# A graph attention edge loop: two PSUM banks in turn for a step's z and its sums, leaky relu as a maximum, transposes in place of identity matmuls

## The reference, cut to what matters

```python
h = relu(layernorm(x))                     # 6250 x 256
xm = h @ W_n2m.T;  ea = edge_attr @ W_r2m.T
# one more loop per node, with the mean of its edges' ea as attribute
xl = xm @ Wl.T + bl;  xr = xm @ Wr.T + br  # 6250 x 128
e = ea_f @ We.T
u = leaky_relu(xl[src_f] + xr[dst_f] + e, 0.2)     # per edge, 8 heads x 16
logits = einsum('ehd,hd->eh', u, att)
alpha = softmax of logits over the edges of one target
out = segment_sum(xl[src_f] * alpha, dst_f) + bias
return x + out @ W_m2n.T
```

## Time and profile before

| | us |
|---|---|
| median of 3 runs | 2426.31 (2423.69 to 2429.64) |
| profiled execution, its own time | 2422.78 |
| its span, first to last instruction | 2421.0 |
| its mean granted TensorE clock | 0.974 of 2.4 GHz |

### The profile page before, as it was taken

How to read it: one execution, slowest core, us unless ns; L and a number is a source line. 1 busy time by engine, 2 the same in 40 slices (tenths; PEclk the granted TensorE clock), 3 DMA queues, 4 the chain that set the end, 5 groups by cost and what they waited for, 6 DMA issues and landing times. The chain is left out here.

```text
span 2421.0 us, 67070 instructions
## 1 busy us (share of the span) xinstructions
PE 2223.0 (92%) x14421; PEld 1609.4 (66%) x14422; DVE 1492.1 (62%) x4173; ACT 1339.9 (55%) x3905; POOL 1722.4 (71%) x1914
## 2 busy tenths in 40 slices
PE   3978999999999999999999999999899999999978
PEld 2745766667766776677666766776677667766656
DVE  4734666656665666566655665666566556666677
ACT  2714555556555655565555655665565556655553
POOL 3777777777777777777777777777777777777501
PEclk9969999999999999999999999999999999999989
DMA  6244444444444444444444544544455445444317
GB/s 200 82 113 112 115 118 111 111 111 121 112 111 112 120 112 110 114 120 113 109 115 114 116 109 115 118 114 108 115 117 114 107 115 118 115 109 112 72 41 134
DMA packets 323471, 272.65 MB, mean 113 GB/s; under 512 B 176135, under 2 KB 294568, under 8 KB 322786
## 3 DMA queue, kind: packets, MB, share of 16 engines
q1 hardware_dynamic: 256686, 144.01, 24.7%
q0 software_dynamic: 60704, 120.20, 21.5%
q10 hardware_dynamic: 5652, 3.68, 0.5%
HBM read 256.21 MB, written 19.40 MB: 114 GB/s over the span
## 5 line engine op out<-in xcount | busy, mean ns | idle before, releaser
L782 POOL DMA_INDIRECT xl_g<-xl_table,src_tab x1708 | 1638.0, 959 | 522.9 <-issue 518.0
L989 DVE SCALAR_TENSOR_TENSOR uT<-banks,relu 128x256 f32<-128x256 f32 x854 | 349.4, 422 | 529.8 <-issue 486.9
L852 PE MATMUL banks<-msg,onehot 128*128 128x177 f32 x3416 | 639.3, 330 | 6.2 <-DVE msg L979 2.3
L902 ACT ACTIVATE relu<-banks 128x256 f32<-128x256 f32 x854 | 319.0, 382 | 582.8 <-PE banks L807 548.5
L852 PEld LDWEIGHTS banks<-msg,onehot 128*128 128x128 f32 x3416 | 522.8, 192 | 172.6 <-issue 163.6
L807 PE MATMUL banks<-ident,xl_g 128*128 128x128 f32 x3416 | 507.1, 293 | 92.1 <-DMA xl_g<-xl_table,src_tab 89.9
L807 PEld LDWEIGHTS banks<-ident,xl_g 128*128 128x128 f32 x3416 | 424.2, 195 | 246.5 <-DMA xl_g<-xl_table,src_tab 168.0
L890 ACT ACTIVATE distance<-iota_n,minus_slot 128x128 f32<-128x128 f32 x1708 | 540.7, 389 | 0.4
L798 PE MATMUL banks<-onehotT,xr_parts 128*128 128x256 bf16 x2562 | 357.4, 276 | 34.9 <-issue 18.1
L895 ACT ACTIVATE onehot<-distance 128x512 f32<-128x512 f32 x427 | 268.9, 630 | 113.1 <-PE banks L852 93.8
L798 PEld LDWEIGHTS banks<-onehotT,xr_parts 128*128 x2562 | 246.0, 98 | 89.4 <-issue 45.3
(11 more groups left out here) (195 smaller groups left out, 1393.9 us busy)
## 6 DMA issues: line engine op xcount, KB each, us to landing
slot_bc<-slot_dram SPq DMA_DIRECT2D x427, 128.0 KB
xl_g<-xl_table,src_tab POOLq DMA_INDIRECT x1708
attrT<-in_attr_cols SPq DMA_DIRECT2D x854, 32.0 KB
rbf<-in_edge_attr SPq DMA_DIRECT2D x854, 32.0 KB
masks<-masks_dram SPq DMA_DIRECT2D x108, 96.5 KB
out<-in_x SPq DMA_DIRECT2D x16, 336.0 KB
out<-result POOLq DMA_DIRECT2D x6, 896.0 KB, 9.2
xl_table<-lr_sb SPq DMA_DIRECT2D x49, 64.0 KB, 1.5
```

What stands on the lines that cost most here:

```text
L782: pool.indirect_dma_start(out=xl_g[:, k % RING, t], out_offset=None, in_=xl_table, in_offset=bass.IndirectOffsetOnAxis(ap=src_tab[:, e:e + ...
L852: mm = nc.tensor.matmul(U_ps[h], onehot[:, j % 2, t], msg[:, j % 2, t], start=i == 0, stop=i == PT - 1)
L902: nc.scalar.activation(relu[:, h], z_ps[h], ACT.Relu, scale=1.0 - SLOPE).then_inc(relu_ready, 2 + h)
L989: nc.vector.scalar_tensor_tensor(out=uT[:, s % 2, h * PIECE:(h + 1) * PIECE], in0=z_ps[h], scalar=SLOPE, in1=relu[:, h], op0=ALU.mult, op1 ...
```

## The change

- z has one bank of 512 columns a step, two banks in turn. Its first matmul waits for z_copied of the step two back.
- The attributes of both pieces lie on the same 32 partitions, and one matmul of 512 columns takes them.
- The gathered rows are turned with is_transpose, still added into z. The finale's turns the same.
- ACT copies z to SBUF (z_copy, two in turn); DVE makes u = max(0.2 z, z) of it, both operands the copy, one operation of 512 columns.
- U of a step has one bank for both pieces, two in turn; the sums are added at SUM_LAG = LAG + 2 instead of LAG + 1, RESCALE moves from turn 9 to 10, and there is one more turn. TensorE waits for the sums of the step two back.
- The ring of slot_bc has 4 steps instead of 8. Semaphores that counted halves now count steps.

```diff
-SRING = 8
+SRING = 4
 LAG = BATCH + 9
+SUM_LAG = LAG + 2
...
-        attrT = sb("attrT", [SPLIT * D_RBF, TRING, PIECE])
-        relu = sb("relu", [P, SPLIT, PIECE])
+        attrT = sb("attrT", [D_RBF, TRING, GROUP])
+        z_copy = sb("z_copy", [P, 2, GROUP])
...
-        z_ps = [banks[:, h, 0:PIECE] for h in range(SPLIT)]
+        z_ps = [banks[:, par] for par in (0, 1)]
...
-        U_ps = banks[:, 2, P:P + AGG], banks[:, 5, 0:AGG]
+        U_ps = [banks[:, 2 + 3 * par, 0:SPLIT * AGG].rearrange("p (h c) -> p h c", h=SPLIT) for par in (0, 1)]
...
-        FORTH, BACK, ENDS, CHAIN, SPREAD, RAISE, TURN, SCALE, RESCALE = 1, 2, 3, 4, 5, 6, 7, 8, 9
+        FORTH, BACK, ENDS, CHAIN, SPREAD, RAISE, TURN, SCALE, RESCALE = 1, 2, 3, 4, 5, 6, 7, 8, 10
...
+                    z = z_ps[s % 2]
                     pe.wait_ge(ohT_ready, k + 1)
+                    if inside(k - 2, STEPS):
+                        pe.wait_ge(z_copied, k - 1)
                     for h in range(SPLIT):
-                        if inside(k - 1, STEPS):
-                            pe.wait_ge(u_ready, Z * (k - 1) + (2, Z)[h])
                         for part in range(PARTS):
-                            nc.tensor.matmul(z_ps[h], parts_of(xr_parts, w[h], part),
-                                             onehotT[:, n4, h * PIECE:(h + 1) * PIECE], start=part == 0, stop=False)
+                            nc.tensor.matmul(z[:, h * PIECE:(h + 1) * PIECE], parts_of(xr_parts, w[h], part),
+                                             onehotT[:, n4, h * PIECE:(h + 1) * PIECE],
+                                             start=h == 0 and part == 0, stop=False)
...
-                    for h in range(SPLIT):
-                        q = slice(h * D_RBF, (h + 1) * D_RBF)
-                        nc.tensor.matmul(z_ps[h], Wc[q], attrT[q, s % TRING], start=False, stop=False)
+                    nc.tensor.matmul(z, Wc[0:D_RBF], attrT[:, s % TRING], start=False, stop=False)
                     pe.wait_ge(gathers[s % RING], (r * (UNROLL // RING) + s // RING + 1) * GATHERED)
                     for h in range(SPLIT):
                         for i in range(PT):
-                            mm = nc.tensor.matmul(z_ps[h][:, i::PT], xl_g[:, s % RING, i * SPLIT + h], ident[:],
-                                                  start=False, stop=i == PT - 1)
-                        mm.then_inc(z_done, 2 + h)
+                            mm = nc.tensor.matmul(z[:, h * PIECE + i:(h + 1) * PIECE:PT], xl_g[:, s % RING, i * SPLIT + h],
+                                                  ident[:], start=False, stop=h == SPLIT - 1 and i == PT - 1,
+                                                  is_transpose=True)
+                    mm.then_inc(z_done, 1)
...
+                    if inside(k - LAG - 2, STEPS):
+                        pe.wait_ge(added, TICK * (k - LAG - 1))
                     for h in range(SPLIT):
-                        if inside(k - LAG - 1, STEPS):
-                            pe.wait_ge(added, TICK * (k - LAG - 1) + (1, TICK)[h])
...
-                    for h in range(SPLIT):
-                        act.wait_ge(z_done, Z * k + (2, Z)[h])
-                        if inside(k - 1, STEPS):
-                            act.wait_ge(u_ready, Z * (k - 1) + (2, Z)[h])
-                        nc.scalar.activation(relu[:, h], z_ps[h], ACT.Relu, scale=1.0 - SLOPE).then_inc(relu_ready, 2 + h)
+                    act.wait_ge(z_done, k + 1)
+                    if inside(k - 2, STEPS):
+                        act.wait_ge(u_ready, k - 1)
+                    nc.scalar.activation(z_copy[:, s % 2], z_ps[s % 2], ACT.Copy).then_inc(z_copied, 1)
...
-                a = k - LAG - 1
+                a = k - SUM_LAG
...
-                    dve.wait_ge(agg_done, TICK * a + 1)
+                    dve.wait_ge(agg_done, a + 1)
...
-                    for h in range(SPLIT):
-                        dve.wait_ge(relu_ready, Z * k + (2, Z)[h])
-                        if h == 0 and inside(k - 2, STEPS):
-                            dve.wait_ge(L_done, k - 1)
-                        nc.vector.scalar_tensor_tensor(out=uT[:, s % 2, h * PIECE:(h + 1) * PIECE], in0=z_ps[h],
-                                                       scalar=SLOPE, in1=relu[:, h], op0=ALU.mult, op1=ALU.add
-                                                       ).then_inc(u_ready, 2 + h)
+                    dve.wait_ge(z_copied, k + 1)
+                    if inside(k - 2, STEPS):
+                        dve.wait_ge(L_done, k - 1)
+                    z = z_copy[:, s % 2]
+                    nc.vector.scalar_tensor_tensor(out=uT[:, s % 2], in0=z, scalar=SLOPE, in1=z,
+                                                   op0=ALU.mult, op1=ALU.max).then_inc(u_ready, 1)
...
-                    nc.tensor.matmul(T_ps[:, i], old[:, b % 2, i], ident[:], start=True, stop=False)
-                    mm = nc.tensor.matmul(T_ps[:, i], own[:, b % 2, i], ident[:], start=False, stop=True)
+                    nc.tensor.matmul(T_ps[:, i], old[:, b % 2, i], ident[:], start=True, stop=False,
+                                      is_transpose=True)
+                    mm = nc.tensor.matmul(T_ps[:, i], own[:, b % 2, i], ident[:], start=False, stop=True,
+                                      is_transpose=True)
```

More of the change, by code:

```diff
@@ L705, in edge_loop @@
         FULL, GATHERED = SPLIT * 16, TILES * 16
-        (set_up, acc_zero, ohT_ready, node_saved, z_done, relu_ready, u_ready, L_done, dist_ready, oh_ready,
+        (set_up, acc_zero, ohT_ready, node_saved, z_done, z_copied, u_ready, L_done, dist_ready, oh_ready,
          attr_ready, msg_ready, agg_done, added, forth_done, run_done, ends_done, seq_ready, seq_half, seq_done,
@@ L709, in edge_loop @@
          last_ready, weight_ready, wT_done, spread_done, factor_ready, rescaled, x_set) = map(sem, (
-             "set_up", "acc_zero", "ohT_ready", "node_saved", "z_done", "relu_ready", "u_ready", "L_done",
+             "set_up", "acc_zero", "ohT_ready", "node_saved", "z_done", "z_copied", "u_ready", "L_done",
              "dist_ready", "oh_ready", "attr_ready", "msg_ready", "agg_done", "added", "forth_done", "run_done",
@@ L720, in edge_loop @@
         SET_UP, ACC_PARTS = 4, 7
-        TICK, Z = 3, 5
-        first, last_turn = -2, STEPS + LAG + 1
+        TICK = 3
+        first, last_turn = -2, STEPS + SUM_LAG
         looped = (4 * BATCH - 1, STEPS - 2)
-        FORTH, BACK, ENDS, CHAIN, SPREAD, RAISE, TURN, SCALE, RESCALE = 1, 2, 3, 4, 5, 6, 7, 8, 9
+        FORTH, BACK, ENDS, CHAIN, SPREAD, RAISE, TURN, SCALE, RESCALE = 1, 2, 3, 4, 5, 6, 7, 8, 10
         def batch_at(s, r, piece):
@@ L749, in _ @@
                     if inside(k - TRING, STEPS):
-                        sp.wait_ge(z_done, Z * (k - TRING + 1))
+                        sp.wait_ge(z_done, k - TRING + 1)
                         sp.sem_inc(z_seen, 1)
                     for h, e in enumerate(edges):
-                        sp.dma_start(attrT[h * D_RBF:(h + 1) * D_RBF, s % TRING], attr_cols[:, bass.DynSlice(e, PIECE)]
+                        sp.dma_start(attrT[:, s % TRING, h * PIECE:(h + 1) * PIECE], attr_cols[:, bass.DynSlice(e, PIECE)]
                                      ).then_inc(turned_in[s % TRING], 16)
@@ L846, in _ @@
                     pe.wait_ge(oh_ready, TICK * (k - LAG + 1))
+                    if inside(k - LAG - 2, STEPS):
+                        pe.wait_ge(added, TICK * (k - LAG - 1))
                     for h in range(SPLIT):
[L848 to L849 removed]
                         for i in range(PT):
                             t = i * SPLIT + h
[L852 removed]
+                            mm = nc.tensor.matmul(U_ps[j % 2][:, h], onehot[:, j % 2, t], msg[:, j % 2, t],
                                                   start=i == 0, stop=i == PT - 1)
[L854 removed]
+                    mm.then_inc(agg_done, 1)
                 b = batch_at(s, r, TURN)
@@ L893, in _ @@
                     if inside(k - LAG - 1, STEPS):
-                        act.wait_ge(agg_done, TICK * (k - LAG))
+                        act.wait_ge(agg_done, k - LAG)
                     nc.scalar.activation(onehot[:, m % 2], distance[:], ACT.Relu, scale=-1.0, bias=1.0
@@ L937, in _ @@
                         dve.wait_ge(acc_zero, ACC_PARTS)
-                    if (s - LAG - 1) % BATCH == 0:
-                        b = r * (UNROLL // BATCH) + (s - LAG - 1) // BATCH
+                    if (s - SUM_LAG) % BATCH == 0:
+                        b = r * (UNROLL // BATCH) + (s - SUM_LAG) // BATCH
                         if inside(b - 1, BATCHES):
                             dve.wait_ge(rescaled, b)
-                    dve.wait_ge(agg_done, TICK * a + 1)
+                    dve.wait_ge(agg_done, a + 1)
+                    sums = U_ps[(s - SUM_LAG) % 2]
                     if inside(a - 1, STEPS):
                         dve.wait_ge(added, TICK * a)
```

(13 more changed lines are left out.)

4 lines of the change are left out of this document (2 added, 2 removed).

## The result

The changed kernel takes 2463.9 us (median of 4, 2459.86 to 2467.63) against 2426.2 for the kernel before (2423.69 to 2429.64): 1.0152 of it, 95% interval 1.0139 to 1.0165. The profiled execution took 2459.86 us, 37.1 more than that of before.

A forecast was written before the change was run, and what follows sets the result against it. GpSimd's 1708 gathers were taken to bound the kernel, with TensorE waiting for them. The profiled 2422.8 us + 36 (maximum) - 2 (drain) - 1 (finale) = 2456, with the median 3.5 above: 2459 us, range 2421 to 2484.

The forecast's parts named there:

- The term of 36 us: Loop: gathers lengthened by the new two-SBUF-input maximum, + 36 us, five sixths of the even-phase 43 us.
- 0.76 + e: Time of a gather starting under a two-SBUF-input DVE operation that ends e later, if over 0.944 us (e over 0.19).
- even phase: Gathers every 1.25 us starting at any phase of the DVE operation: mean loss (D - 0.19)^2 / 2.5, 43 us for the maximum.
- The discount of a sixth: Maximum's landing relative to the next gather spreads somewhat to the harmless side: 36 us taken, five sixths of even.
- The check on the kernel before: Whole trace before: lengthening by scans, raises, product and compare worked out by the law as 26.5 us, against 25.6 seen.
- Rival 1: Maximum: same address twice may be read once, or only scans and raises collide; no lengthening, 2423 us (2416 to 2427), 14%.
- Rivals 2 and 3: Gathers' phase locked to the maximum: harmless, + 4 to 10 us, 2430, 6%; or harmful, + 85 us, 2508, 8%.
- two terms: TensorE a step: attributes' matmul +0.18 us, net gain with transposes 0.3 to 0.4, hidden by gathers; spare time 0.64 us.
- 0.64 us a step in hand: TensorE's spare time in the loop: a turn of 4.35 us when behind, against the gathers' 4.99 us a step.
- rival 4: TensorE's clock: fewer passes, more standing, more low-clock turns; at half of them + 243 us, 2670 us, 4%.
- The 2 us for the drain: Seventeen turns after the last gather: sums no longer wait for the same turn's matmuls, gain 0 to 6 us, 2 taken.
- The finale's 1 us: Finale: transposes halve the last batch's 28 bare passes, saving 2.1 us, of which ACT's steps leave about 1.

The follow-up runs named there:

- the useless operation: Kernel before plus one unread DVE maximum of iota_n with itself a step, 512 columns, both inputs in SBUF: 2474.4 us, ratio 1.0202.
- the slow chip: Changed kernel with the maximum's first operand, forth and seq_forth in PSUM, on a chip where the kernel before took 3516 us: 3296 us, ratio 0.9381.

## Why the prediction was right

It gave 2459 us, 2421 to 2484, slower with 0.8; 2463.9 came out. Its signs of being right came too: a gather's median is still 944 ns, the mean 981, busy 1675.8 us, the last one at 2320.2.

*The bound.* Held. GpSimd's idle time is 523.0 us, before 522.9; gathers set the time, and the difference of the spans is that of the gathers to 1 us.

*The maximum.* The mechanism is as forecast. The term of 36 us measured 44.4 under the maximum itself, at 0.40 of the steps and 0.26 us each. Other operations lost 6.6 us less, so gathers grew by 37.8; that this is so near 36 is luck. What was mis-sized is the constant. Behind the maximum a gather takes 0.82 + e, not 0.76 + e, so the lengthening begins at e = 0.944 - 0.82 = 0.12 and not at 0.19. With this, even phase gives (0.696 - 0.12)^2 / 2.5 x 427 = 57 us instead of 43, and the trace has 44.7 (all gathers that start under a maximum with more than 0.12 us left), 0.79 of it. The discount of a sixth "to the harmless side" was about right; the full loss that it was taken from was a quarter too small. The 0.76 holds for the scans from which it was read.

The check on the kernel before, 26.5 us worked out against 25.6 seen, was closer than its parts, too: its trace has 18.9 us under the three scans, where 16.2 were worked out, and 2.4 under the compare L955, where 5.5 were.

*Rival 1* (one and the same address) falls with the trace of the changed kernel and with the useless operation in the kernel before, whose two inputs are one tile as well. Rivals 2 and 3 (locked phase) fall with the count: 0.40 of the maxima is what even phase gives, and the starts lie over the whole length of the operation. They are not quite even, 28 of the 171 start with 0.60 to 0.64 us left.

*TensorE.* Here two terms were mis-sized, and only the cover hid it. The transposes save 0.49 us a turn, near the 0.54 put down for them; the matmul on one set of rows costs 0.42, not 0.18, so that TensorE gained 0.07 and not 0.3 to 0.4. And "0.64 us a step in hand" was read from a plain turn. With the batch's pieces the mean turn of before, when TensorE is behind, is about 5.24 - 0.42 = 4.82 us (an estimate from the run with one set of partitions) against 5.05: 0.23 in hand. The one matmul eats more than that, and the transposes pay for it: without them the change costs 3%, as measured, which no rival had.

*The clock* (rival 4). It fell from 0.974 to 0.940, and the rows above show a turn of 6.70 us (1441.58 to 1448.28) after 1.38 us of standing. The ring took it up: GpSimd waited 4.0 us for msg in all, and the run with the maximum from PSUM lost nothing at 0.947. In every profiled execution with transposes in the loop the mean was 0.936 to 0.952, in every other 0.967 to 0.977, the slow chip left out. The Trainium skill says ("TensorE: Matmul & The Clock Gate", Part 4) that transposes aren't counted as busy in the same way. That would fit; but TensorE also stands longer for gathers where its turn is short, and no run parts the two. That the full clock doesn't engage for transposes, as the same sentence has it, isn't so in this stream of matmuls and transposes: from 1448 to 1453 us the granted clock is 1.00 of 2.4 GHz, and the four transposes take 0.66 us, where they took 1.12 at 1441.58.

*Drain and finale.* The 2 us for the drain didn't come: U of a step waits for the sums of the step two back, but DVE makes these in the same turn as it made those of one back. The idle time moved, from L945 (252.3 to 90.1 us at L947) to the wait for the copy. The finale's 1 us came, though not by the sum given for it. Its last batch did 14 passes instead of 28, but in 2.71 us (2444.72 to 2447.43), where the 28 took 3.20 (2407.66 to 2410.86). Timeline of TensorE after, then before:

```profile
2444.72 0.30 PE L1205 MATMUL banks<-ident,old 128*128 128x128 f32 x1 [2.90 <-DVE old L1317]
...
2445.30 0.42 PE L1205 MATMUL banks<-ident,old 128*128 128x128 f32 x1
2445.51 0.42 PE L1207 MATMUL banks<-ident,own 128*128 128x128 f32 x1
...
2447.43 3.71 PE L1214 MATMUL banks<-W_outT,gatT 128*128 128x256 f32 x14
```

```profile
2410.86 3.19 PE L1210 MATMUL banks<-W_outT,gatT 128*128 128x256 f32 x14
```

Most of the 14 start 0.21 us apart, where the 28 started 3.20 / 28 = 0.11 apart: the granted clock was 0.72 on average from 2444 to 2450 us, after TensorE had stood 2.90 us, and 1.00 from 2407 to 2414 us in the kernel before.

*What held the gathers.* The rule of the Trainium skill, "SBUF — State Buffer", section "Who interferes with whom", that two SBUF inputs contend with a GpSimd instruction that reads SBUF, agrees with the runs: 1.42 us under a maximum and 0.95 under the same with one operand in PSUM. Its inference that tensor_tensor doesn't hold up descriptor generation doesn't hold for these gathers: L1044, a tensor_tensor with both inputs in SBUF, ran from 305.16 to 305.44 in the run with the attributes on one set of partitions, and the gather that started at 305.19 took 1.07 us, 0.82 over its rest. That it is the gather's read of src_tab that waits is argued, not shown. Nor are two SBUF inputs needed in every case: the bf16 compare L955 has one, and gathers that start under it lose 2.4 us in the kernel before.

## What to carry to other kernels

Where indirect gathers on GpSimd set the pace, look at every DVE operation with two operands in SBUF. One of length D costs, at even phase, about (D - 0.12)^2 / 2 over the gathers' spacing (1.25 us here), in us. That is an estimate from these runs: it gives 57 us for the maximum, which lost 44.7, and 55 us for the useless operation, which lost 56.0. So cut such an operation in pieces, or put one operand in PSUM, and don't trade a PSUM operand for an SBUF copy to save DVE time that nobody waits for. An engine's time in hand is read from a mean that holds its rare long turns, not from a plain one. Parts of a change that look idle may pay for one another: test each alone on the kernel before, and each taken out of the changed one.

## What the runs showed of the hardware that was not expected

- One and the same tile as both operands counts as two inputs: gathers lost 44.4 us under the maximum of z_copy with itself, and 55.6 us under that of iota_n with itself.
- A gather isn't held if it starts together with the operation: 31 gathers of the changed kernel that started within the first 0.04 us of a maximum took 0.94 us, and these maxima took 0.72 to 0.77 us, where most take 0.69.
- A gather that waits goes on between two operations that follow each other: the one at 423.58 ended 0.82 us behind the end of the first half.
- Two matmuls of 32 rows on different rows of TensorE, into different banks, run side by side: 303.4 / 427 = 0.71 us a step for both. On the same rows they take 492.1 / 427 = 1.15 us, and the turn grows from 4.35 to 4.78 us.
